# Attention kernel: score tiles sent out singly, interleaved with one key tile of scores and one of sums

## What is computed

```python
qkv = (x @ w_qkv).reshape(B, L, 3, H, Dh)          # B=4, L=1024, H=16 heads, Dh=8
attn = jnp.einsum('bhid,bhjd->bhij', q, k) * scale
attn = attn + phi_bias(L)[None, None]
attn = jax.nn.softmax(attn, axis=-1)
out = jnp.einsum('bhij,bhjd->bhid', attn, v)
```

## Time and profile before

| | |
|---|---|
| median of 3 runs | 1120.49 us (1118.1 to 1120.71) |
| profiled execution, its own time | 1122.93 us |
| its span, first to last instruction | 1121.1 us |
| mean granted TensorE clock | 0.947 |
| busy: TensorE matmul, weight load | 980.0 us (87%), 548.3 us (49%) |
| busy: VectorE, ScalarE, GpSimd | 911.8 us (81%), 726.9 us (65%), 358.1 us (32%) |

### The profile page before, as it was taken

The page is one execution under the profiler, slowest core; times in us unless marked ns, Lnnn a source line. Parts: engine busy times, 40 slices in busy tenths (PEclk is TensorE's granted clock), DMA queues, the critical chain, the costliest instruction groups (busy, mean ns, idle before and its releaser), DMA issues. The chain is left out here.

```text
span 1121.1 us, 36169 instructions
## 1 busy us (share of the span) xinstructions
PE 980.0 (87%) x11663; PEld 548.3 (49%) x11667; DVE 911.8 (81%) x1801; ACT 726.9 (65%) x1573; POOL 358.1 (32%) x468
## 2 busy tenths in 40 slices
PE   5529998574999999999999999999999998639996
PEld 4429998340333333333333333333333346639996
DVE  6447886547999999999999999999999976548885
ACT  1114443470888888888888888888888884224443
POOL 1623444003232323232332323232333323524343
PEclk9999999695899999999999999999999997569998
DMA  9612221686122222222222222222222444622220
GB/s 305 239 63 67 67 66 35 171 278 171 51 72 72 69 69 60 75 73 60 74 64 71 72 64 69 69 69 69 61 76 71 103 106 171 236 71 71 63 67 26
DMA packets 84957, 106.70 MB, mean 95 GB/s; under 512 B 15835, under 2 KB 68065, under 8 KB 84368
## 3 DMA queue, kind: packets, MB, share of 16 engines
q1 hardware_dynamic: 79344, 93.51, 28.7%
q0 software_dynamic: 5568, 12.63, 3.2%
HBM read 74.14 MB, written 36.55 MB: 99 GB/s over the span
## 5 line engine op out<-in xcount | busy, mean ns | idle before, releaser
L1126 DVE TENSOR_REDUCE nmax<-psS 128x1 f32<-128x1024 f32 x512 | 600.7, 1217 | 39.1 <-PE psS L979 31.5
L1269 ACT ACTIVATE big<-psE 128x512 f32<-128x512 f32 x1024 | 553.0, 598 | 101.5 <-PE psE L964 98.9
L964 PE MATMUL psE<-qop,kop 122*32 122x512 bf16 x4096 | 319.0, 386 | 4.5 <-ACT big L1269 3.0
L1341 POOL TENSOR_TENSOR big<-big,const 128x512 f32<-128x512 f32 x128 | 162.7, 1271 | 443.2 <-ACT big L1269 443.2
L997 PE MATMUL psV<-big,vst 128*9 128x256 f32 x4096 | 265.9, 379 | 1.3
L979 PE MATMUL psS<-maxop 32*128 32x512 bf16 x1024 | 176.7, 395 | 28.3 <-DVE nmax L1126 13.3
L997 PEld LDWEIGHTS psV<-big,vst 128*9 128x9 f32 x4096 | 101.4, 90 | 115.7 <-issue 12.4
L964 PEld LDWEIGHTS psE<-qop,kop 122*32 122x32 bf16 x4096 | 90.7, 96 | 132.0 <-ACT big L1269 59.7
L979 PEld LDWEIGHTS psS<-maxop 32*128 32x128 bf16 x1024 | 48.0, 91 | 188.7 <-issue 114.6
L733 ACT ACTIVATE siga<-psGa,w1sa 128x128 f32<-128x128 f32 x156 | 44.6, 368 | 61.0 <-PE psGa L645 61.0
L733 ACT ACTIVATE sigb<-psGb,w1sb 128x128 f32<-128x128 f32 x156 | 44.6, 368 | 60.7 <-PE psGb L645 60.7
(11 more groups left out here) (190 smaller groups left out, 924.9 us busy)
## 6 DMA issues: line engine op xcount, KB each, us to landing
maxop<-qk_parts SPq DMA_DIRECT2D x256, 64.0 KB, 1.9
qop<-qk_parts SPq DMA_DIRECT2D x64, 144.0 KB
kop<-qk_parts SPq DMA_DIRECT2D x64, 144.0 KB
weighted_sums<-osum SPq DMA_DIRECT2D x64, 128.0 KB
qk_parts<-part SPq DMA_DIRECT2D x16, 384.0 KB, 3.6
xsa<-sorted_a SPq DMA_DIRECT2D x39, 128.5 KB, 2.1
xsb<-sorted_b SPq DMA_DIRECT2D x39, 128.5 KB
w1a<-in_w SPq DMA_DIRECT2D x1, 4128.0 KB
```

The costliest lines, as they stand in the source:

```text
L964: last = nc.tensor.matmul(psE[BANK[turn]][32 * c:32 * c + 32, :], kop[b][0:TROWS, lo:lo + 32], qop[b][0:TROWS, half * HALF:(half + 1) * HALF],
L1126: nc.vector.tensor_reduce(nmax[r % 2][:, qt:qt + 1], psS[n % 2][:], AX.XY, ALU.max, negate=True).then_inc(s_max, 1)
L1269: nc.scalar.activation(prob[r % 2][:, lo:lo + HALF], psE[BANK[16 * (r % NBUF) + n]][:], ACT.Exp).then_inc(s_exp, 1)
L1341: nc.gpsimd.tensor_tensor(dst, dst, diag[:, 4 * h:4 * h + 4, :], ALU.mult).then_inc(s_diag, 1)
```

## The change

TensorE's order within a quarter becomes score, weigh, gather of one key tile, twice over. `gather` takes one key tile in place of two, with its waits moved to the tiles where they belong (first tile: values and the copy of `psV`; first and fifth: probabilities and diagonal). On ScalarE the copy of `psV` is issued ahead of the step's first exponential, where it was behind it. The number of matmuls, exponentials, copies, reductions and DMAs is the same.

```diff
-                def gather(p):
-
-                    if p == 0:
+                def gather(k):
+
+                    if k == 0:
                         pe.wait_ge(s_vst, i)
                         if r % 2 == 1 and later(at, -1, 1):
                             pe.wait_ge(s_ev, 2 * q + (r - 1) // 2)
-                    if p in (0, 2):
-                        pe.wait_ge(s_diag, 2 * i - 1 + p // 2)
-                        pe.wait_ge(s_exp, 16 * i - 8 + 8 * (p // 2))
+                    if k in (0, 4):
+                        pe.wait_ge(s_diag, 2 * i - 1 + k // 4)
+                        pe.wait_ge(s_exp, 16 * i - 8 + 8 * (k // 4))
                     side = (r + 1) % 2 * QUART
-                    for k in (2 * p, 2 * p + 1):
-                        for c in range(4):
...
-                    if p == 3:
+                    if k == KT - 1:
                         last.then_inc(s_pv, 1)
 
                 for p in range(4):
+                    if live(at, 2):
+                        score(2 * p)
                     if live(at, 0):
                         weigh(2 * p)
+                    if live(at, -1):
+                        gather(2 * p)
                     if live(at, 2):
-                        score(2 * p)
                         score(2 * p + 1)
                     if live(at, 0):
                         weigh(2 * p + 1)
                     if live(at, -1):
-                        gather(p)
+                        gather(2 * p + 1)
...
                 for n in range(16):
+                    if n == 0 and r % 2 == 1 and live(at, -2):
+                        act.wait_ge(s_pv, i - 1)
...
+                        nc.scalar.copy(osum[s][:], psV[:]).then_inc(s_ev, 1)
                     if live(at, 0):
                         act.wait_ge(s_t, 16 * i + n + 1)
...
-                    if n == 0 and r % 2 == 1 and live(at, -2):
-                        act.wait_ge(s_pv, i - 1)
...
-                        nc.scalar.copy(osum[s][:], psV[:]).then_inc(s_ev, 1)
```

More of the change, by code:

```diff
@@ L989, in gather @@
                             pe.wait_ge(s_ev, 2 * q + (r - 1) // 2)
-                    if p in (0, 2):
-                        pe.wait_ge(s_diag, 2 * i - 1 + p // 2)
-                        pe.wait_ge(s_exp, 16 * i - 8 + 8 * (p // 2))
+                    if k in (0, 4):
+                        pe.wait_ge(s_diag, 2 * i - 1 + k // 4)
+                        pe.wait_ge(s_exp, 16 * i - 8 + 8 * (k // 4))
                     side = (r + 1) % 2 * QUART
-                    for k in (2 * p, 2 * p + 1):
-                        for c in range(4):
[L996 to L999, removed]
-                    if p == 3:
+                    for c in range(4):
+                        at_c = k * PBLK + c * QUART
+                        last = nc.tensor.matmul(
+                            psV[32 * c:32 * c + VW, side:side + QUART], vst[(r + 1) % 2][:, k, :],
+                            prob[(r + 1) % 2][:, at_c:at_c + QUART], start=(k == 0), stop=(k == KT - 1))
+                    if k == KT - 1:
                         last.then_inc(s_pv, 1)
                 for p in range(4):
+                    if live(at, 2):
+                        score(2 * p)
                     if live(at, 0):
                         weigh(2 * p)
+                    if live(at, -1):
+                        gather(2 * p)
                     if live(at, 2):
-                        score(2 * p)
                         score(2 * p + 1)
@@ L1262, in step @@
                 for n in range(16):
+                    if n == 0 and r % 2 == 1 and live(at, -2):
+                        act.wait_ge(s_pv, i - 1)
+                        s = (r - 3) // 2 % 2
+                        if later(at, -3, 4):
+                            act.wait_ge(s_os[s], 32 * (q + (r - 3) // 4))
+                        nc.scalar.copy(osum[s][:], psV[:]).then_inc(s_ev, 1)
                     if live(at, 0):
@@ L1270, in step @@
                                              ACT.Exp).then_inc(s_exp, 1)
-                    if n == 0 and r % 2 == 1 and live(at, -2):
-                        act.wait_ge(s_pv, i - 1)
-                        s = (r - 3) // 2 % 2
-                        if later(at, -3, 4):
-                            act.wait_ge(s_os[s], 32 * (q + (r - 3) // 4))
-                        nc.scalar.copy(osum[s][:], psV[:]).then_inc(s_ev, 1)
                     if at is not None and n % 4 == 3:
```

## The result

The changed kernel takes 1155.45 us, the median of 4 runs (1154.27 to 1156.39), against 1119.81 us (1118.1 to 1120.71, 4 runs) before. The ratio is 1.032, with a 95% interval of 1.0301 to 1.0338: 35.6 us slower. The forecast was 1148.0 us, in a range of 1131 to 1162.

What follows compares the result with a forecast made beforehand. TensorE was to replace the score-reduction ring as bound: 10.32 + 0.27 (copy) = 10.59 us a step against 10.11, +0.48 over 61 steps = +29.0, less 1.5 at the end: 1120.5 + 27.5 = 1148.0 us, range 1131 to 1162.

Steps and rivals of the forecast that it cites:

- the ring of second score and reduction: Old order: a pair's second score starts only when a reduction ends, and reductions wait for score; 10.11 us a head.
- the new bound: TensorE becomes the bound in the new order, at 10.32 us a step before the copy, above VectorE's 9.55.
- about 1 us: Sign in the profile after: VectorE's idle time grows to about this much a head, all released by score.
- Entry from a gather into score: TensorE's extra time going from a gather to a score: taken as 0.10 us, not held in the trace before.
- Rival 2: Going from gather to score on TensorE costs nothing: 9.79 us a step, 1099.5 us in all, faster; chance 0.11.
- Half a quarter: TensorE's new order: score 0.31, weigh 0.45, one-tile gather 0.43, entry into next score 0.10; sum 1.29 us, eight a step.
- The pair: Two scores together on TensorE: the second costs 0.10 us; taken apart, 0.31 us extra a pair, 1.24 a head.
- TensorE had 1.1 us a head to spare: Old order: TensorE's own work is 9.04 us a step, from quarters of 2.26, against 10.11 us a head.
- The copy: ScalarE's copy of `psV` makes TensorE's gather stand 0.53 us every second head, 0.27 a head; ends 0 and 0.35.
- Rival 1: TensorE is the bound but the copy of `psV` does not stall it: 10.32 us a step, 1132 us; chance 0.13.
- Costed at nothing: Put at 0 us: gather's moved waits, the maxima's route (GpSimd, transpose, SyncE transfers), the sums on SyncE's queue, `psE`'s three banks.
- The ends: Last steps without scores: quarters go from 2.18 to 1.96 us, giving back up to 1.8 us, taken as 1.5.

## Why the prediction was right

**What bounds it.** Right: the ring of second score and reduction, and the new bound. Halving the reductions sped the old order up by 69 us and left the loop of the new one as it was. VectorE's idle time before its reductions went from 29.6 to 37.6 us between 400 and 900 us, 0.6 to 0.8 us a head, in the direction forecast and short of the "about 1 us".

**Entry from a gather into score.** Taken as 0.10, bounds 0 and 0.11; measured 0.11, the upper one. The Trainium skill (TensorEngine Tiling (Array Packing), Key Properties) says that changing the tiling mode drains TensorE. The trace agrees: 0.54 us from a gather to score, 0.43 to a weigh, which has the gather's 32-column strips. The trace gives the price, and no run here separates a drain from another cause of it. Rival 2, at 1099.5 us, needed under 0.04.

**Half a quarter.** Forecast 1.29, measured 1.30. On eight halves and 61 steps this 0.01 is 5 us. The term is "eight are 10.32 us", too small by 0.08: four figures each read to 0.01 us and added up before they were multiplied by 488. With the copy 0.02 too large and the bank of 0.02 left out, a step is 10.67 against 10.59. The profiled executions account for 3.8 of the 7.5 us between forecast and result (+31.3 against +27.5 us on the span: +5.2 from the steps, -1.4 from the ends); the rest is where they lie among their runs, the one before 2.4 us above the median known then, the one after, at 1154.27, 1.2 below its own.

**The pair.** The price of taking one apart was put at 0.31 us, with 0.10 for its second score. It is 0.32 + 0.11 - 0.01 = 0.42, and 4 x 0.42 is the 1.68 us between 8.72 and 10.40. This reading was wrong, and it was luck of the method that it did not touch the forecast, which counted the new order directly and had no pair in it. It did touch the expectation for the halved reductions (1072 against 1051.2 us) and the sentence that TensorE had 1.1 us a head to spare: by the 2.18 us quarter it had 10.11 - 8.72 = 1.39. So the loss adds up: 1.68 paid, less 1.39 to spare, and 0.27 for the two stalls are the 0.56 us a head.

**The copy.** Forecast 0.53 us every second head, measured 0.50; the run with the copy behind moved it to 1.30 and the time to 1180.97 us, where 1180 was expected. Rival 1, that it costs nothing, is out by the profile: the gather is late at 26 of the 27 copies between 300 and 880 us. That the stall would go with a later gather was expected too, and there waits for banks took back 0.16 of the 0.25 us a head.

**Costed at nothing.** Held: the waits for diagonals, the maxima's route and SyncE's queue show in none of the long waits. The banks nearly held: once in four heads one costs 0.08 us, 0.02 a head. They would not have with the weighs 0.43 us closer, as the late gather showed.

**The ends.** Forecast -1.5 us, measured -2.9, which is all that lies outside the 61 steps. The quarter at the end came out at the 1.96 us forecast, which is good for up to 1.8; where the rest lies is open. Outside the loop both kernels also have stretches at the lower clock (granted clock 0.50 between 260 and 280 us in both), and what these add was not separated.

## What to carry to other kernels

Cost a reordering by start-to-start distances in stretches without waits, and by which neighbours each instruction gets; the busy share stayed at 98% while the work done per microsecond fell by 5%. Where two pieces of work of one kind, like the scores, overlap each other and not their neighbours, a pair costs as much as one, and spreading them evenly pays the price twice. Evening out the supply of the next engine pays only while its price stays within what the engine that pays has to spare: here 1.68 us a head against 1.39, for 0.6 us of VectorE's idle time. And when a change makes an engine the bound, every small stall that its slack used to cover comes due: the copy's stall, free in the old order, cost 0.25 us a head in the new one.

## What the runs showed of the hardware

Each of the four matmuls of two scores has its weights on other 32 rows, and the second score adds 0.01 us when its buffer is free: 0.33 us from the first of four matmuls to the next weigh against 0.32 from the first of two. In the earlier trace rows it looked like 0.10. The shortest distance in a trace need not be the engine's own time while another engine is still in the ring: taking that engine out showed it, and so does the end of the reduction, 0.06 us ahead of the second score.
